# Summing the high bands' taps on ScalarE and GpSimd ahead of one centring product each

## What is computed

```python
low = x
for _ in range(NUM_LEVELS):
    lens.append(low.shape[1])
    l = dwconv(low, h_filter)[:, ::2]
    h = dwconv(low, g_filter)[:, ::2]
    highs.append(h)
    low = l
low = linear_attention(low, NUM_HEADS)
for h, L in zip(reversed(highs), reversed(lens)):
    up_l = jnp.repeat(low, 2, axis=1)[:, :L]
    up_h = jnp.repeat(h, 2, axis=1)[:, :L]
    low = dwconv(up_l, h_synth) + dwconv(up_h, g_synth)
return layer_norm(x + low, norm_gamma, norm_beta)
```

## Time and profile before

| what | value |
|---|---|
| time, median of 3 runs | 206.12 us (205.91 to 206.71) |
| profiled execution, from first to last instruction | 204.6 us |
| PE busy | 181.2 us, 89% |
| DVE busy | 125.5 us, 61% |
| POOL busy | 127.5 us, 62% |
| ACT busy | 90.3 us, 44% |

### The profile page before, as it was taken

The page is one execution under the profiler, slowest core; times in us unless marked ns, Lnnn a source line. Parts: engine busy times, 40 slices in busy tenths (PEclk is TensorE's granted clock), DMA queues, the critical chain, the costliest instruction groups (busy, mean ns, idle before and its releaser), DMA issues.

```text
span 204.6 us, 3620 instructions
## 1 busy us (share of the span) xinstructions
PE 181.2 (89%) x1196; PEld 156.4 (76%) x1196; DVE 125.5 (61%) x430; ACT 90.3 (44%) x239; POOL 127.5 (62%) x195
## 2 busy tenths in 40 slices
PE   6979898999979999998999999999999999957800
PEld 6947688999936677857899999999999889945700
DVE  4888999999878787785667644454445344422300
ACT  0687512448697768110344344444444345422210
POOL 7494005556117475927777888878878777866660
PEclk9999999999999999999999999999999999995875
DMA  5599999800030271104313323333233333332221
GB/s 149 182 411 419 420 419 419 363 12 3 0 117 0 99 225 51 49 23 138 91 44 42 43 42 45 54 40 42 43 47 53 40 40 29 40 40 21 20 24 13
DMA packets 11649, 22.26 MB, mean 109 GB/s; under 512 B 1504, under 2 KB 8800, under 8 KB 11504
## 3 DMA queue, kind: packets, MB, share of 16 engines
q1 hardware_dynamic: 5968, 17.52, 22.7%
q0 software_dynamic: 5664, 4.53, 16.1%
HBM read 17.72 MB, written 4.33 MB: 108 GB/s over the span
## 4 chain that ended last, share of the span: by engine, by line
PE 41%; DMA 15%; POOL 14%; issue 11%; DVE 10%; ACT 4%; POOLq 1%; SPq 1%; DVEq 0%; ACTq 0%
DMA out_dram<-area,rows 13%; POOL out_dram L542 9%; PE bank L1155 7%; PE bank L1434 4%; PE bank L1110 4%; PE bank L1435 4%; POOL hT L531 4%; PE bank L1296 4%; PE bank L1415 3%; PE bank L1308 3%; DMA x_tok<-in_x_dram 2%; PE bank L1258 2%; DVE junk L950 1%; DVE area L807 1%; DVE hT L817 1%
## 5 line engine op out<-in xcount | busy, mean ns | idle before, releaser
L542 POOL DMA_INDIRECT out_dram<-area,rows x32 | 50.7, 1584 | 16.8 <-DMA out_dram<-area,rows 8.7
L1086 DVE SCALAR_TENSOR_TENSOR area<-bank,consts,sgate 128x256 f32<-128x256 f32 x64 | 30.9, 483 | 42.4 <-ACT sgate L734 42.1
L734 ACT ACTIVATE sgate<-bank,consts 128x256 f32<-128x256 f32 x64 | 30.3, 473 | 53.3 <-PE bank L1435 53.1
L1434 PE MATMUL bank<-area,wT 128*128 128x256 f32 x128 | 40.3, 397 | 4.8 <-issue 4.1
L1415 PEld LDWEIGHTS bank<-wT,area 128*128 128x128 f32 x256 | 38.1, 191 | 4.1 <-DVE area L1086 1.0
L531 POOL DMA_INDIRECT hT<-h_rows,rows x32 | 31.9, 995 | 12.7 <-issue 9.1
L1435 PE MATMUL bank<-area,wT 128*128 128x256 f32 x128 | 39.3, 390 | 0.0
L1415 PE MATMUL bank<-wT,area 128*128 128x128 f32 x256 | 38.6, 275 | 0.6 <-DVE area L1086 0.6
L1435 PEld LDWEIGHTS bank<-area,wT 128*128 128x128 f32 x128 | 25.2, 197 | 3.7
L1434 PEld LDWEIGHTS bank<-area,wT 128*128 128x128 f32 x128 | 20.5, 198 | 6.2 <-issue 5.7
L518 POOL TENSOR_TENSOR sh_hid<-sh_up,sgate 128x64 f32<-128x64 f32 x48 | 13.7, 322 | 14.6 <-ACT sh_up L686 12.1
(11 more groups left out here) (195 smaller groups left out, 259.1 us busy)
## 6 DMA issues: line engine op xcount, KB each, us to landing
wT<-in_weights_dram SPq DMA_DIRECT2D x16, 768.0 KB, 16.2
h_rows<-hrow SPq DMA_DIRECT2D x2, 576.0 KB, 3.7
x_tok<-in_x_dram SPq DMA_DIRECT2D x4, 256.0 KB, 3.9
x_tok<-in_down_b_dram SPq DMA_DIRECT2D x1, 1024.0 KB, 6.2
out_dram<-x SPq DMA_DIRECT2D x4, 256.0 KB, 2.1
hT<-h_rows,rows POOLq DMA_INDIRECT x32, 2.6
out_dram<-area,rows POOLq DMA_INDIRECT x32
sh_wT<-in_shared_dram SPq DMA_DIRECT2D x1, 384.0 KB, 2.9
```

The costliest lines, as they stand in the source:

```text
L542: pool.indirect_dma_start(out=out_rows, in_=eo[:, e % 2, c, :], in_offset=None, out_offset=bass.IndirectOffsetOnAxis(ap=rows[:, c, e:e + 1 ...
L734: act.activation(sgate_e[:, q % SGB, :], up_bank(q)[:, CAP:2 * CAP], ACT.Silu, bias=biasT[:, 1, j, e:e + 1]).then_inc(s_sil, 1)
L1086: dve.scalar_tensor_tensor(hidden[:, e % 2, j, :], up_bank(q)[:, 0:CAP], biasT[:, 0, j, e:e + 1], sgate_e[:, q % SGB, :], ALU.add, ALU.mul ...
L1434: pe.matmul(up_bank(q)[:, 0:CAP], wT[:, e, 0, j, :], xselT[:, e % 2, :], start=True, stop=True)
```

## The change

TensorE no longer filters the high band. For each batch, ScalarE makes five scaled copies of the shifted band (`products`, 128x512 each), GpSimd adds three of them to the even tokens' sum and two to the odd tokens' (`high_bands`, three additions of 128x512), and `synth2_high(n)` makes one product with the centring matrix for each tile: four for a group, not ten. The high band of batch 1 leaves VectorE: ScalarE makes its four scaled copies, and GpSimd adds them in three additions into `h1p`. So GpSimd gets nine additions of 128x512 in all, and ScalarE fourteen scaled copies for five diagonal matrices. The scaled copies share five buffers, which a count of uses (`s_used`) hands back from GpSimd to ScalarE. `synth2_high` stands at other places of TensorE's program, and 12 `stay_warm` products stand where the first of them stood. In the code `pool`, `act`, `dve` and `pe` are GpSimd, ScalarE, VectorE and TensorE.

```diff
+        scaled = [v[:, t, :] for v in (sh_up, sgate) for t in range(2)] + [x1T[:, 0, :]]
+        high_sum = xn_tok[:, :, :].rearrange("p i c -> p (i c)").rearrange("p (b r n) -> p b r n", b=NB, r=2)
...
+        HIGH_AT = (0, 1, 2, 1, 2)
+        USES = {1: (1, 1, 1, 1, 1), 2: (2, 2, 2, 3, 3)}
...
...
                 last = pool.tensor_tensor(by_x[n][:, :], part[n][:, 0, :], part[n][:, 1, :], ALU.add)
             last.then_inc(s_masks, 1)
+            def add(dst, a, b):
+                return pool.tensor_tensor(dst, a, b, ALU.add)
+            pool.wait_ge(s_prod, 2)
+            link(add(scaled[0], scaled[0], scaled[1]))
+            pool.wait_ge(s_prod, 4)
+            link(add(scaled[2], scaled[2], scaled[3]))
+            last = add(h1p[:, 1, 1:N1 + 1], scaled[0], scaled[2])
+            last.then_inc(s_h1p, 1)
+            pool.wait_ge(s_h1p, 1)
+            pool.sem_inc(s_used, 1)
+            def high_bands(b):
+                done = 4 + 5 * b
+                pool.wait_ge(s_prod, done + 2)
+                link(add(high_sum[:, b, 0, :], scaled[0], scaled[1]))
+                pool.wait_ge(s_prod, done + 3)
+                link(add(high_sum[:, b, 0, :], high_sum[:, b, 0, :], scaled[2]))
+                pool.sem_inc(s_used, 1)
+                pool.wait_ge(s_prod, done + 5)
+                link(add(high_sum[:, b, 1, :], scaled[3], scaled[4]))
+                pool.sem_inc(s_used, 1)
+                pool.sem_inc(s_high, 1)
+            high_bands(0)
+            high_bands(1)
             pool.wait_ge(s_xna, NB)
...
+            def products(first, src, scales):
+                for k, scale in enumerate(scales):
+                    if first:
+                        act.wait_ge(s_used, USES[first][k])
+                    act.activation(scaled[k], src(k), ACT.Copy, scale=scale).then_inc(s_prod, 1)
...
+            act.wait_ge(s_xp, 4)
+            products(0, phase_src, [taps[:, 4 + k:5 + k] for k in LATE_FIRST])
             act.wait_ge(s_comb, 1)
-            act.wait_ge(s_centre, 1)
-            diagonals(diag_c[:, 5:10, :], centre[:, :], [tap_sum(1, k) for k in range(5)])
             act.wait_ge(s_h1, 1)
             act.copy(h1p[:, 0, 1:N1 + 1], bank[4][:, :]).then_inc(s_h1a, 1)
-            diagonals(diag[:, 6:8, :], ident[:, :], [tap_sum(1, k) for k in (3, 4)])
-            diagonals(diag[:, 4:6, :], ident[:, :], [tap_sum(0, k) for k in (3, 4)])
+            act.wait_ge(s_h1a, 1)
+            products(1, high_src(0), [tap_sum(1, k) for k in range(5)])
             act.wait_ge(s_l2, 1)
             act.activation(expf[:, :], l2f[:, :], ACT.Exp).then_inc(s_exp, 1)
...
             act.copy(kT[:, :], bank[7][:, :]).then_inc(s_kT, 1)
+            diagonals(diag[:, 6:8, :], ident[:, :], [tap_sum(1, k) for k in (3, 4)])
+            diagonals(diag[:, 4:6, :], ident[:, :], [tap_sum(0, k) for k in (3, 4)])
+            act.wait_ge(s_h1p, 1)
+            products(2, high_src(1), [tap_sum(1, k) for k in range(5)])
...
             finish_even(0)
-            for k in range(3):
-                link(high1(k))
-            high1(3).then_inc(s_h1v, 1)
             finish_even(1)
...
+            def synth2_high(n):
+                pe.wait_ge(s_high, n // 2 + 1)
+                pe.wait_ge(s_centre, 1)
+                for t in range(4):
+                    b, par, m0, dst = place(n, t)
+                    pe.matmul(dst, high_sum[:, b, par, m0:m0 + P], centre[:, :], start=False, stop=False,
+                              skip_group_check=True)
...
             add_xn(1)
-            synth2_high(0)
-            synth2_high(1, range(2))
+            stay_warm(12, bank[5])
             pe.wait_ge(s_l2, 1)
...
             last.then_inc(s_kv, 1)
-            synth2_high(1, range(2, 4))
+            synth2_high(0)
             pe.wait_ge(s_kvm, 1)
```

More of the change, by code:

```diff
@@ L214, in wavelet_attention_moe @@
         s_h1a = sem("s_h1a")
-        s_h1v = sem("s_h1v")
+        s_h1p = sem("s_h1p")
+        s_prod = sem("s_prod")
+        s_used = sem("s_used")
+        s_high = sem("s_high")
         s_h2 = sem("s_h2")
@@ L604, in _, with high_src, phase_src @@
             keep_xp(1, 1)
+            def products(first, src, scales):
[3 more added lines that the diff above has]
+                    act.activation(scaled[k], src(k), ACT.Copy, scale=scale).then_inc(s_prod, 1)
+            def high_src(b):
+                return lambda k: h1p[:, b, HIGH_AT[k]:HIGH_AT[k] + N1]
+            LATE_FIRST = (1, 3, 0, 2)
+            def phase_src(j):
+                r, o = PHASE[LATE_FIRST[j]]
+                return xp[:, r, 1, o:o + N1]
+            act.wait_ge(s_xp, 4)
+            products(0, phase_src, [taps[:, 4 + k:5 + k] for k in LATE_FIRST])
             act.wait_ge(s_comb, 1)
[L606 to L607 removed]
             act.wait_ge(s_h1, 1)
             act.copy(h1p[:, 0, 1:N1 + 1], bank[4][:, :]).then_inc(s_h1a, 1)
[L610 to L611 removed]
+            act.wait_ge(s_h1a, 1)
+            products(1, high_src(0), [tap_sum(1, k) for k in range(5)])
             act.wait_ge(s_l2, 1)
@@ L821, in level1_even @@
                                                 ALU.mult, ALU.add)
[L823 to L828, removed]
             low2 = l2f[:, :].rearrange("p (b n) -> p b n", b=NB)
@@ L1157, in synth @@
                 return last
[L1159 to L1162, removed]
+            def synth2_high(n):
[5 more added lines that the diff above has]
+                              skip_group_check=True)
             def synth2_low(n):
-                pe.wait_ge(s_diag, 5)
+                pe.wait_ge(s_diag, 4)
                 pe.wait_ge(s_r1v, n // 2 + 1)
@@ L1206, in _ @@
             pe.wait_ge(s_h2, 1)
-            pe.wait_ge(s_diag, 3)
+            pe.wait_ge(s_diag, 2)
             pe.wait_ge(s_h1a, 1)
@@ L1210, in _ @@
                 synth1_odd(b, h2p, 6)
+            synth2_high(1)
             for b in range(NB):
@@ L1215, in _ @@
                 last.then_inc(s_attnT, 1)
-            pe.wait_ge(s_diag, 4)
+            synth2_high(2)
+            pe.wait_ge(s_diag, 3)
             pe.wait_ge(s_apv, 1)
@@ L1230, in turn_x1 @@
                 last.then_inc(s_x1Tp, 1)
-            synth2_high(2)
+            synth2_high(3)
             synth2_low(2)
             turn_x1(0)
-            synth2_high(3)
             synth2_low(3)
```

1 line of the change is left out of this document (added).

## The result

| | before | after |
|---|---|---|
| time, median (lowest to highest) | 206.25 us (205.91 to 206.71), 4 runs | 216.56 us (216.03 to 219.11), 4 runs |
| ratio, 95% interval | | 1.052 (1.047 to 1.057): slower |
| profiled execution, first to last instruction | 204.6 us | 214.3 us |
| DVE busy | 125.5 us | 131.6 us |
| POOL busy | 127.5 us | 140.9 us |

The change costs 10.3 us. Forecast were 7.9 us (214.0), within 209.0 to 217.0. A run that lasts over 1.5% longer than the fastest of the same kernel stands in no median and no ratio here (two of e4_short_adds, 210.78 and 211.47 us, and one of e11_short_warm, 468.45 us).

The account below looks back on a forecast made before the run. VectorE was taken to bound the tail, behind a head of dependent steps. Head +6.6, clock +1.7 and tail -0.4 gave +7.9 us on the profile's 204.6: 212.5, or 214.0 as median, within 209.0 to 217.0.

Parts of the forecast that it names:

- The bound: Tail: VectorE, 96% busy, sets the pace; time follows from `synth2_low(0)`'s start (33.31) plus 5.22 us to line 903.
- steps 1 to 3: Head: GpSimd adds and VectorE take turns; exponential 3.6 us later, keys times values 5.0, second high band 5.2.
- Step 4, even tokens: Head: adds 7 and 8 hold VectorE's even tokens by 0.9 us; division at 34.5 instead of 28.42, +6.1.
- Step 5, groups 1 and 2 on TensorE: Head: group 1's matmuls cost 0.3 us at most, group 2's wait +0.2; `synth2_low(0)` at 39.9, +6.6.
- The clock in the head: Head: TensorE's 4.8 us gap drops the grant to 0.50, slowing matmuls on the path: +1.7 us.
- The tail's gain: Tail: without `high1`, line 903 comes 0.4 us earlier, as it still waits for GpSimd's power.
- All behind follows at VectorE's pace and then in a chain with nothing parallel to catch up.: Tail behind line 903: any delay there carries through unchanged; TensorE's 3.6 us of removed matmuls costed at nothing.
- if VectorE has gaps in the tail: Tail: one of three signs that would show the forecast wrong; VectorE was expected 96% busy there.

Follow-up runs that it names:

- e4_short_adds: changed kernel with GpSimd's nine additions over 8 of 512 columns and 7 more warm products in the tail's gap; 207.91 us, ratio 1.009.
- e11_short_warm: changed kernel with additions over 8 columns and more warm products: 16 for 12, 4 ahead of the second turn, 7 in the tail; 208.77 us, ratio 1.011.
- e10: kernel before without the 40 high-band matmuls of groups 2 and 3, with 7 warm products in the gap this opens; 206.40 us, ratio 1.001.
- e8: kernel before without VectorE's four operations for batch 1's high band (`high1`); 206.03 us, ratio 0.999.
- e9: changed kernel with 28 warm products for 12, 7 more in the tail and 8 more ahead of the second turn of the queries; 216.55 us, ratio 1.049.
- e3: changed kernel with 28 warm products for 12 in the head and 7 more in the tail's gap; 213.76 us, ratio 1.035.
- e7: kernel before without the 40 high-band matmuls of groups 2 and 3, gap not filled; 208.49 us, ratio 1.011.
- e1: changed kernel with 7 more warm products (14 matmuls) in the tail's gap behind the first router products; 214.66 us, ratio 1.041.

## Why the prediction was right, point by point

**The bound.** Right as far as the last new x. Line 950 starts 4.84 us behind the odd tokens' end (forecast 4.8), and from 46.15 VectorE goes from group to group as before (line 950 again at 49.44 and 52.79), busy for 12.16 of the 12.65 us to 58.80, which is the 96% of the forecast. e10 shows that the 40 matmuls alone were worth nothing. But TensorE is nearly as full: in e8, VectorE's 0.37 us did not reach the end.

**Holds, steps 1 to 3.** Right in mechanism, and nearly in size. Adds 1 to 3 end at 19.19, 20.86 and 22.27, with the 0.29 us by which this execution got there earlier at 19.5, 21.2 and 22.6; forecast were 19.5, 21.1 and 22.5. The exponential is 3.71 late (3.6). It is ScalarE's queue that sets this, not the held input, which the prediction had a little later still: three adds and not four hold that input, and it is there at 24.39. The copies follow at 0.615 us (22.41 to 25.48 for five), not 0.56. The queries end at 27.48 and not at 23.49, with the 0.29 us 4.3 later (forecast 5.1): the first of their two operations is held while the second still waits for the exponential, so that only one hold counts. The next add holds line 873 behind them instead (1.49 us for 0.48). So the second high band on VectorE ends at 28.93 + 2.33 = 31.26, which is 5.3 later (5.2).

The Trainium skill's GPSIMD Engine Reference (§ 1, Specifications) says that GpSimd shares its SBUF interfaces with VectorE and contends with VectorE's instructions that have two SBUF inputs or run in a two-port mode. The trace agrees and adds the price: 0.88 us an operation for 512 columns. No row shows in which mode an operation ran. The trace also shows that a small operation is held no less. Line 899's two operations have 16 columns; ns of one (least, median, most), first and last start:

```profile
L899 DVE TENSOR_SCALAR kvz<-same,bank x2: 240/778/1315, 31.6 to 31.7; 128x16 f32<-128x16 f32 x2
```
For the add itself, the figure of § 3.1 of that page in the Trainium skill (Elementwise — side-by-side cycle accounting; 4497 ns for 2048 columns) had given an estimate of 1.12 us; the shortest ones here take 1.27.

**Step 4, even tokens.** Mis-sized. The prediction has adds 7 and 8 hold "VectorE's even tokens by 0.9 us". But adds 7 to 9 hold three operations in a row, and all three stand ahead of the division: the mask (line 899, 1.47 for 0.39), and lines 902 (1.35 for 0.48) and 877 (1.68 for 0.76), together 2.87 us. The prediction counted one hold there, not three. Of the 2.87, 0.2 fill the 0.23 us for which line 857 waited before. The division is 8.3 late (36.41; 28.42 in the earlier trace rows), not 6.1.

**Step 5, groups 1 and 2 on TensorE.** Forecast 0.5 us, measured nothing: the odd tokens are late by the same 8.3 as the division.

**The clock in the head.** The dip is there, 0.50 after a gap of 3.88 us, but its term is mis-sized: 0.3 us of waiting before the mask in the changed kernel, 0.44 by e9, against 1.7. The prediction's own words, "less what VectorE's held steps hide", were the point, and it took too little off. So the head's 8.3 us came out right by luck, by errors that cancel: 5.3 + 0.3 + 2.7 in place of 5.2 + 0.9 + 0.5 + 1.7.

**The tail's gain.** 0.37 us at line 950 for a forecast of 0.4. e8 shows that `high1` alone brings none of it to the end, since TensorE is full behind it. With the 40 matmuls gone too, the gain stays (e3).

**What failed.** "All behind follows at VectorE's pace and then in a chain with nothing parallel to catch up." It does so until the last x. But the chain then runs over TensorE, and TensorE, freed of its work, waits 1.83 us for x, falls to 1.2 GHz, and puts 14 filling products at half clock ahead of the turn. That is 2.4 of the 2.6 us between 214.0 and 216.6. The prediction costed the freed time at nothing, and its clock term stood in the head alone. The freed time was a loss, as e7 shows alone and e3 and e10 show by its absence. Among the prediction's own signs of being wrong was "if VectorE has gaps in the tail", and VectorE's 2.33 us of waiting for the logits is such a gap: the total lies in the range, but this step of the mechanism failed.

## What to carry to other kernels

A GpSimd operation on long float32 rows is priced by whom it holds: count each VectorE operation that runs beside it, small ones too, and ask which of them lie on the path. Where two engines are about equally full, work taken from one is worth nothing, and a relieved TensorE can lose its clock: look at the granted clock behind each place where a change leaves it waiting, and put filling products where nothing that is awaited stands behind them (no run here tried that). A term for the clock is to be taken only for the time in which TensorE, and not a held neighbour, ends last.

## What the runs showed of the hardware

- Doing 40 matmuls less made the kernel before 2.4 us slower (e7), through gaps of 1.83 and 0.75 us in TensorE's work and a grant of 0.50 for the 6 us behind them.
- The same 14 filling products kept the clock at 1.00 in e3 and e10, and not in e1 and e9 (e1: 0.67 and 0.50 from 56 to 60 us; e9: 0.72 from 56 to 62). Only the granted clock of the run itself tells.
- A VectorE operation of 128x16 was held by a GpSimd add at least as long as one of 128x512: it took 1.3 us for some 0.2, so it was held by 1.1 us (line 899), against 0.88.
